# A two-layer recurrent network with routed experts on one core: a new way to pick two experts, one table for exp and log, and the first steps reordered

## The reference, cut to what matters

```python
x = L0_attn_hidden_states                     # 8 x 512 tokens x 128
xn = layernorm(x)
s = L0_attn(xn)      # q, k, v: projection + short conv + silu; then a scan over 32 chunks of 16 tokens
g = silu(L0_moe(xn)) # softmax over 8 logits, top 2 experts, weights p1/(p1+p2), p2/(p1+p2)
x = x + s * g
xn = layernorm(x)
s = L1_ssm(xn)       # state-space scan, 16 states x 256 channels, softplus(delta), exp(delta * A)
g = silu(L1_moe(xn)) # the same routing, but each expert keeps only its first 1.25 * S / 8 tokens
x = x + s * g

# one chunk of the layer-0 scan ("step"); W_in and W_out are 4 x 8 per head, carried on
k_h = softmax(k_t . W_in) * lr;  q_h = softmax(q_t . W_in)
qk = (q_h . k_h) * causal_mask
o_t = q_h . W_out + qk . v_t
W_out = W_out + k_h^T v_t
for _ in range(2):
    g_out = -attn(W_in, k_t, v_t);  g_in = -attn(W_out, v_t, k_t)
    W_in = W_in - lr_in * g_in;     W_out = W_out - lr_out * g_out
```

## Time and profile before

| | us |
|---|---|
| median of 3 runs | 1341.43 |
| lowest, highest | 1332.81, 1348.08 |
| the profiled execution, its own time | 1332.28 |
| span in the profile | 1330.5 |
| DVE busy in the span | 1225.3 (92%) |
| PE, ACT, POOL busy | 1007.2, 720.2, 700.2 |

### The profile page before, as it was taken

How to read it: one execution, slowest core, us unless ns; L and a number is a source line. 1 busy time by engine, 2 the same in 40 slices (tenths; PEclk the granted TensorE clock), 3 DMA queues, 4 the chain that set the end, 5 groups by cost and what they waited for, 6 DMA issues and landing times. The chain is left out here.

```text
span 1330.5 us, 15939 instructions
## 1 busy us (share of the span) xinstructions
PE 1007.2 (76%) x3654; PEld 583.8 (44%) x3655; DVE 1225.3 (92%) x2277; ACT 720.2 (54%) x1364; POOL 700.2 (53%) x637
## 2 busy tenths in 40 slices
PE   4865347887778878887677587569899889898874
PEld 2512334555555555555545542233444444444431
DVE  7997899999999999999997779999989899989999
ACT  5654015555565455654434556446667666766741
POOL 5038732333333333333210027789879778878885
PEclk9687558898999899998877588889999899999988
DMA  9749141000000000000162124464445444443346
GB/s 305 216 119 307 57 134 43 20 24 18 21 24 18 23 18 21 24 18 18 53 203 64 32 107 126 144 177 154 149 146 187 159 136 175 161 155 141 137 150 191
DMA packets 106771, 145.49 MB, mean 109 GB/s; under 512 B 26347, under 2 KB 82424, under 8 KB 101856
## 3 DMA queue, kind: packets, MB, share of 16 engines
q1 hardware_dynamic: 90816, 114.51, 27.2%
q0 software_dynamic: 10240, 25.32, 5.9%
q10 hardware_dynamic: 5664, 5.11, 1.3%
HBM read 112.26 MB, written 39.04 MB: 114 GB/s over the span
## 5 line engine op out<-in xcount | busy, mean ns | idle before, releaser
L2123 DVE TENSOR_TENSOR ps<-ps,cv 128x512 f32<-128x512 f32 x256 | 162.8, 681 | 2.4 <-DMA cv<-bc_scr 2.4
L1161 PE MATMUL ps<-Q,ident 128*128 128x512 f32 x206 | 115.4, 652 | 25.9 <-DVE Q L2141 15.1
L985 PE MATMUL ps<-wd_a,xn 128*128 x576 | 93.8, 312 | 42.7 <-ACT xn L1372 42.7
L1390 ACT ACTIVATE x<-x 128x128 f32<-128x128 f32 (+1 forms) x127 | 32.2, 278 | 140.7 <-DVE x L1981 69.1
L965 PE MATMUL ps<-wg_a,xnT 128*128 x144 | 92.6, 729 | 17.2 <-issue 10.8
L782 POOL DMA_INDIRECT y_tok<-xnT,meta x72 | 72.5, 1006 | 60.6 <-ACT xnT L1378 47.9
L985 PEld LDWEIGHTS ps<-wd_a,xn 128*128 128x128 f32 x576 | 78.9, 212 | 56.3 <-issue 54.8
L995 PE MATMUL ps<-x,ident 128*128 128x64 f32 x512 | 73.6, 296 | 28.8 <-DMA wu_a<-in_wu_a 11.9
L760 POOL DMA_INDIRECT slots_x<-xn,sl_put x64 | 74.9, 1170 | 37.7 <-issue 18.9
L791 POOL TENSOR_TENSOR xn<-xn 128x512 f32<-128x512 f32 x24 | 30.3, 1262 | 122.0 <-DVE x L1944 96.9
L995 PEld LDWEIGHTS ps<-x,ident 128*128 128x128 f32 x512 | 72.9, 217 | 43.2 <-issue 33.1
(11 more groups left out here) (383 smaller groups left out, 3049.1 us busy)
## 6 DMA issues: line engine op xcount, KB each, us to landing
cv<-bc_scr SPq DMA_DIRECT2D x64, 512.0 KB, 3.9
xn<-bc_scr SPq DMA_DIRECT2D x24, 1024.0 KB, 4.7
O<-bc_scr SPq DMA_DIRECT2D x8, 1024.0 KB, 4.9
slots_x<-O POOLq DMA_DIRECT2D x28, 260.0 KB, 5.6
qkv_scr<-wg_a SPq DMA_DIRECT2D x24, 256.0 KB, 3.6
xnT<-slots_x SPq DMA_DIRECT2D x72, 64.0 KB
x<-in_x SPq DMA_DIRECT2D x8, 512.0 KB, 6.5
y_tok<-slots_x SPq DMA_DIRECT2D x2, 2048.0 KB, 13.5
```

The costliest lines, as they stand in the source:

```text
L985: m = pe.matmul(ps[:, 0, 0:D], hidT[:, k, f * P:(f + 1) * P], wd_a[:, bass.ds(off + f * D, D)], start=(f == 0), stop=(f == FC - 1))
L1161: pe.matmul(ps[:, 4, :], ident[:], yc_of(c, n), start=(n == 0), stop=(n == NS - 1)).then_inc(y0_used, 1)
L2123: tt(dBu(g), ps[:, 2 + g, :], b_rows[:, n % 4, :], ALU.mult).then_inc((inject0, b_used)[g], 1)
```

## The change

- **Dispatch.** The two experts are picked from the logits: the row maximum, a one-hot of the first place that has it (`down_e` holds 8 to 1, so that the maximum of mask times `down_e` marks the first), the same again with the first expert pushed down by -3e38. Only the gap between the two maxima is exponentiated (128x32 in place of 128x256), and the weights are 1/(1+e) and e/(1+e). Layer 1 adds a large number to dropped slots instead of multiplying with a kept mask. The expert indices (`texp_i`) are computed behind the slots.
- **One table.** `natural_log_exp_and_others` is loaded where the exp table was, so a log between two exps needs no switch.
- **Projection stage.** `norms` runs in pairs as the squares come; the masks' `ranks(0)` stands between the two halves of the K norms; PE multiplies the units 20 to 23 one by one between the pairs of the Q norms; `unit_length_root(0)` moves behind the convolutions; the gate matmuls have seven banks; V is loaded in three parts.
- **Leading steps.** PE waits for the expert weights only before step 3; POOL makes `op_of` of steps 0 to 3 and `pq_of` of steps 1 to 3, between its scatters, before numbers 5, 16 and 27 of the second 32 (`LEADING`). In step 3 `o_sums` goes ahead of the first expert tiles.
- **Every step.** WO is gone. W_out stays where the running sum leaves it: PP is made from `ends`, the last column of the rows of CS and SC (a stride of 17 numbers, 68 bytes), and one copy (L1940) is left out.
- **Layer 1.** `ranks(1)` goes ahead of the third inner projection.

```diff
+        CS_SC = r.take(2 * DI * HD, CH + 1)
+        CS, SC = CS_SC[:, 0:DI * HD], CS_SC[:, DI * HD:]
+        ends = CS_SC[:, :, CH].rearrange("p (D e) -> p D e", e=HD)
...
-                o.mark(dve.tensor_copy(WO[:, 0, :], CS[:, :, CH]))
-                w_o = o.mark(dve.scalar_tensor_tensor(WO[:, 1, :], GR[:, 3], lr_of(1, c), CS[:, :, CH], ALU.mult, ALU.add))
+                w_o = o.mark(dve.scalar_tensor_tensor(SC[:, :, CH], GR[:, 3], lr_of(1, c), CS[:, :, CH], ALU.mult, ALU.add))
                 dve.wait_ge(v_packed, c + 1)
                 o.wait(w_o)
-                tt(PP, bc(VC, 1, 2 * DI), bc(both(WO[:]), 2, CH), ALU.mult).then_inc(p2_ready, 1)
+                tt(PP, bc(VC, 1, 2 * DI), bc(ends, 2, CH), ALU.mult).then_inc(p2_ready, 1)
...
+                def one_hot(j, src, top):
+                    o.link(tt(eq, src, bc(top, 2, E), ALU.is_equal))
+                    o.link(tt(eq, eq, bc(down_e[:], 1, NT), ALU.mult))
+                    o.link(dve.tensor_reduce(pick, eq, AX_X, ALU.max))
+                    o.link(tt(oh[:, j], bc(down_e[:], 1, NT), bc(pick, 2, E), ALU.is_equal))
+                o.link(dve.tensor_reduce(first, lg, AX_X, ALU.max))
+                one_hot(0, lg, first)
+                o.link(dve.scalar_tensor_tensor(others, oh[:, 0], LOWEST, lg, ALU.mult, ALU.add))
+                o.link(dve.tensor_reduce(second, others, AX_X, ALU.max))
+                tt(gap, second, first, ALU.subtract).then_inc(logits_ready, 1)
+                one_hot(1, others, second)
+                tt(mask, oh[:, 0], oh[:, 1], ALU.add).then_inc(mask_ready, 1)
...
-            for b in range(4, B):
-                project(2 * B + b)
             pe.wait_ge(lr_copied, B)
-            norms(1, sq_q, 7)
+            for k in range(4):
+                project(2 * B + 4 + k)
+                norms(1, sq_q, 7, (k,))
...
-            for b in range(B):
-                silu(2 * B + b)
-                if b < 4:
-                    tap(2 * B + b + 4)
-                k = b - 2
-                if 0 <= k < 4:
-                    if k == 0:
-                        act.wait_ge(q_in, 32)
-                    square(Q, sq_q, 2 * k)
+            act.wait_ge(q_in, 32)
+            for k in range(4):
+                silu(2 * B + k)
+                tap(2 * B + 4 + k)
+                square(Q, sq_q, 2 * k)
+            for b in range(4, B):
+                silu(2 * B + b)
...
                 for i in range(NT):
+                    if j and i in LEADING:
+                        o_product(LEADING.index(i))
+                        q_product(LEADING.index(i) + 1)
...
-            pe.wait_ge(slots_ready, 1)
-            pe.wait_ge(we_loaded, 16 * 3)
...
                 q_sums(c, 4, HD)
+                if after and not here:
+                    o_sums(c)
...
-                    if k == 0:
+                    if k == 0 and (here or not after):
                         o_sums(c)
             with pe.Fori(0, FIRST - 1) as c:
                 step(c, False)
+            pe.wait_ge(slots_ready, 2)
+            pe.wait_ge(we_loaded, 16 * 3)
```

More of the change, by code:

```diff
@@ L548, in op_of, with heads_load @@
             return eng.tensor_tensor(OP, bc(EQ, 2, HD), CS.rearrange("p (D e) l -> p D e l", D=DI)[:, :, :, 1:CH + 1], ALU.mult)
[L550 to L556, removed]
+        def heads_load(eng, lo, hi, w, dst, done):
+            for b in range(lo, hi):
+                eng.wait_ge(stored[b], 16 * ((1, 0, 2).index(w) + 1))
+            eng.dma_start(dst[lo * H:hi * H, :, :],
+                          qkv_scr[w, lo:hi].rearrange("b (h e) t -> (b h) e t", h=H)).then_inc(done, 16)
         block = ctx.enter_context(nc.Block())
@@ L910, in project, with norms @@
                 pe.matmul(ps[:, 2 + cu % 4, :], wproj[:, w * P:(w + 1) * P], xnT[:, b * L:(b + 1) * L], start=True, stop=True).then_inc(proj_ps, 1)
[L912 to L917, removed]
+            def norms(n, sq, bank, pairs):
+                for k in pairs:
+                    pe.wait_ge(squared, 4 * n + k + 1)
+                    for e in (2 * k, 2 * k + 1):
+                        m = pe.matmul(ps[:, bank, :], ident[:], sq[:, e, :], start=(e == 0), stop=(e == HD - 1))
+                if k == 3:
+                    m.then_inc(norm2, 1)
             turn0(0)
@@ L1235, in _ @@
             inner(0, 1)
+            ranks(1)
             pe.wait_ge(conv1_done, 2)
@@ L1316, in _ @@
             silu(2 * B - 1)
-            act.preload_act_table(ACT.Exp)
+            act.wait_ge(k_in, 32)
+            for k in range(2):
+                square(K, sq_k, 2 * k)
+            act.preload_act_table_set(EXP_AND_LOG)
             act.wait_ge(logits_ready, 1)
-            act.activation(route[0].lg, route[0].lg, ACT.Exp).then_inc(probs_ready, 1)
-            act.wait_ge(k_in, 32)
-            for k in range(4):
+            act.activation(best[:, 2, :], best[:, 2, :], ACT.Exp).then_inc(probs_ready, 1)
+            for k in range(2, 4):
                 square(K, sq_k, 2 * k)
@@ L1347, in _ @@
             act.activation(LR[:], LR[:], ACT.Ln, bias=1.0).then_inc(lr_log, 1)
-            act.wait_ge(lr_stored, 16)
-            for b in range(B):
-                act.wait_ge(gate_ps, b + 1)
-                act.activation(gateT[:, b * L:(b + 1) * L], ps[:, 2 + b % 4, :], ACT.Copy).then_inc(gate_copied, 1)
-            act.preload_act_table(ACT.Exp)
-            act.wait_ge(v_in, 32)
+            for b in range(3, B - 1):
+                gate(b)
+            act.preload_act_table_set(EXP_AND_LOG)
+            gate(B - 1)
             temper = HD ** -0.5
@@ L1420, in step @@
                     exp(E2, rec_2, exp_2, temper)
-                if after:
+                if after and here:
                     xT(c + 1, 0)
@@ L1431, in step @@
                     y(c, 0)
+                if after and not here:
+                    xT(c + 1, 0)
                 if after:
@@ L1747, in dispatch @@
-                o.wait()
-                tt(mask, oh[:, 0], oh[:, 1], ALU.add).then_inc(mask_ready, 1)
+                eq, others = prod[:, 0], prod[:, 1]
+                first, second, gap, pick = (best[:, n, :] for n in range(4))
+                def one_hot(j, src, top):
[3 more added lines that the diff above has]
+                    o.link(tt(oh[:, j], bc(down_e[:], 1, NT), bc(pick, 2, E), ALU.is_equal))
@@ L1858, in _, with step @@
             tt(E3[:, DI:2 * DI, :], SK, bc(M3[:, DI:2 * DI], 2, CH), ALU.subtract).then_inc(rec_3, 1)
-            def step(c, routed, first=False, last=False, alone=False, early=None, late=None):
+            def step(c, routed, first=False, last=False, early=None, late=None):
                 ts = bass.ds(c * CH, CH)
@@ L1874, in step @@
                 o.wait(o.n)
-                if alone:
+                if first:
                     pq_of(dve, c).then_inc(pq_ready, 1)
@@ L1982, in step @@
                 gated(2)
-            dve.wait_ge(v_in, 32)
-            PER_R = PER_P = 27
-            step(0, False, first=True, alone=True)
+            dve.wait_ge(v_in, 48)
+            PER_R = PER_P = 26
+            step(0, False, first=True)
             for lo, hi, routed in ((1, FIRST, False), (FIRST, AFTER, True)):
@@ L1991, in _ @@
                     o.loop(c, first - lo * per, per)
-                    step(c, routed, alone=not routed)
+                    step(c, routed)
                 o.end(first, per, hi - lo)
```

146 lines of the change are left out of this document (70 added, 76 removed).

## The result

The changed kernel takes 1349.05 us (median of 20 runs, 1344.09 to 1354.28) against 1338.29 for the kernel before (20 runs, 1329.66 to 1348.08): ratio 1.0082, 95% interval 1.0065 to 1.0099, 11 us slower. The forecast was 1337 us. The time lies in its range and within 1%, but the sum said 4.5 us less and the runs say 11 us more; that difference of some 15 us is what the rest explains.

What follows compares the result with a forecast made beforehand. DVE was taken to bound the steps, so edits count on its chain. Terms +21 - 3 + 1 - 12.5 - 3 + 3.5 - 3 - 8.5 = -4.5 us, put on the median 1341.4: 1337 us, range 1317 to 1350.

Steps and rivals of the forecast that it cites:

- PP read in place: In each step PP reads W_out at a 68-byte stride: +21 us, the copy left out -3, strided updates +1.
- The order of w_c and h_k: In every step w_c now stands ahead of h_k; the prediction had no term for this.
- First stage: Before step 0, convolutions and gate copies end earlier and step 0's wait for expert weights goes: -12.5 us.
- the closed circle of the units 20 to 23: Before step 0, tap, square, norms and next projection form rounds of 4.6 us; convolutions end at 98.3: -4.3 us.
- Rival 2: Circle of units 21 to 23 with PE at its lower level, rounds of 7.2 us: +3.5, 1345 us; chance 0.17.
- Leading steps: Before step 4, four `op_of` and three `pq_of` leave DVE, which then waits for ACT's exp: -3 us.
- Step 3 to 4: In step 3 ACT's copies for the first tiles stand ahead of step 4's exp: +3.5 us.
- -3 for dispatch: In layer 1 mask, ranks and slots get shorter, the softplus chain loses two loads and the ranks: -3 us.
- -8.5 for the rows: In layer 1's rows, four of six DVE stalls for exp lose at most 2.56 us each: -8.5 us (3 to 10).
- Rival 3: Table switches are worth 2.66 us each, with a drain of 1.38: -10, 1331 us; chance 0.07.

Runs made afterwards that it cites:

- e3: The changed kernel with the strided operand kept and h_k ahead of w_c again: 1342.29 us, ratio 1.0057 to the kernel before.
- e5: On the changed kernel with packed WO and old order (ratio 0.9876), POOL's products of the first four steps moved among the scatters: 1321.18 us, ratio 0.9894.
- e8: On the changed kernel with packed WO and old order (ratio 0.9876), step 3's old order of exp, first tiles and o sums: 1317.24 us, ratio 0.9856.
- e10: The changed kernel without the table set in the rows of the second layer: 1353.96 us, ratio 1.0139 to the kernel before.
- e4: The changed kernel with the products of the first four steps on DVE again, POOL making none between its scatters: 1345.57 us, ratio 1.0070.

## Why the prediction was wrong

By its own steps, the forecast in us, then what was measured:

- **PP read in place, +21 - 3 + 1 = +19**: right. PP at 1903 ns for 1.90; all three together 17 us by the ratios, 19 by the step.
- **The order of w_c and h_k, nothing**: this is the step that failed. The full diff has it, the swapped lines and a new `o.wait(w_c)` (the cut diff above leaves them out), and the prediction gives it no term. It costs 0.32 us in a step, 10 us: some 6 are the wait that reading in place forces on x_k, and so part of the price of the term above, and 4 are a swap that nothing forced (e3). By the sequencer's records both are dear because a register instruction for the address stands behind the wait. Together with the term above a routed step was forecast at 19.0 us and is 19.37.
- **First stage, -12.5**: right, mechanism and size. Step 0 starts 6.4 to 7.8 us earlier and the 5.4 us wait is gone; the closed circle of the units 20 to 23 has its forecast round. Rival 2 (a circle at PE's low clock) did not come: the granted clock from 85 to 120 us was 0.86, not 0.70. Its price was read wrong, too: at the low level the row it names has 2.06 us for two records, 1.03 and not 0.85 each, so that a round would have taken 8.1 us and not 7.2 (6 x 1.03 + 1.9).
- **Leading steps, -3**: wrong in sign. Three instructions stretched by 2.76, 1.72 and 1.21 us eat the 4.8 us of the seven products, and DVE waits 0.38 us for exp in three steps. Taking it back gave 1.6 and 2.4 us by the ratios, 3 us by the profiles. I had asked only whether POOL would be late. The Trainium skill (SBUF — State Buffer, "Who interferes with whom") says that a VectorE instruction with two SBUF inputs contends with a GpSimd one that reads SBUF, and that `tensor_reduce` does not; the rows of the changed kernel and of e5 agree, and with that rule the sign of the term would have been open.
- **Step 3 to 4, +3.5**: right in kind and near in size: the wait is 2.9 us. Taking it back (e8) gave 2.7 us by the ratios and 2.6 by the profile up to step 4, but only 0.4 up to step 31, so the net size is between 0.4 and 3 us.
- **Layer 1, -3 for dispatch and -8.5 for the rows**: the two together are 5 to 7 us, and nearly all of it is the table set. The -3 came, but from the set: without it (e10) the way from logits to scan is 27.1 us, as before. The shorter dispatch gave 0.4 us there, and DVE waits 8.3 us for the softplus instead of 2.7 in e10:

```profile
DVE K L2120 <- ACT V L1632: 8.3, 1, 8.3
```

  The rows gave some 2 to 4 us of the forecast 8.5. It counted each load as if the exp behind it were released by nothing else; the exps are released by PE's low-rank product too. The forecast took the 15.0 us of one row of waits down to 6; that row is 10.4, and all four rows together stayed at 21.

Sum with the measured sizes: +17 + 10 - 12 + 2 + 3 - 6 = +14 (with the step 3 term at its most), against 11 and 13.5 measured (1.0082 and 1.0101). Of the 18 us between this sum and the forecast's, 10 are the order, 5 the leading steps and 5 the loads, less 2 for PP. That the time still lies in the range is luck: its slow end was there for rival 2 (1345 to 1350 us), which did not come, and nothing in it stood for the order.

Rival 3 falls by its price. In both kernels every load in the rows starts 17 to 19 ns behind the ACTIVATE ahead of it and takes 1.28 us, and the next ACTIVATE, where it has nothing else to wait for, starts 11 to 12 ns behind it. So a switch is 1.31 us here, and the drain of 1.38 us that the Trainium skill adds (ScalarE: Activation LUTs, "What ACT_TABLE_LOAD costs") does not show.

## What to carry to other kernels

On an engine that is busy 96% of a stage, an edit of the order of small dependent instructions is an edit of the time: look, for each instruction, whether the one directly ahead of it makes its input, and whether its own address is computed behind that wait. Saving a copy by reading and writing in place can cost twice, in the strided operand and in the new write-after-read wait (x_k must not overwrite what w_c still reads); this change paid a third time for a swap that it didn't need. And before work is moved from DVE to POOL, look at what DVE does at that moment: beside reductions the products here were free for DVE, beside products of two SBUF tiles each cost DVE 1.1 to 1.7 us for a length of 1.1 to 1.2.

## What the hardware showed

- A DVE TENSOR_TENSOR beside a POOL TENSOR_TENSOR lasts until 0.10 us (64 elements) or 1.1 us (1024 elements) behind its end: 1.37 us for 0.22, 2.94 and 3.98 for 1.22. It stands as one long busy row, and no wait names it. By the starts of the records DVE's instruction began first each time (137.00 against 137.64), and it was still the one that was held.
- POOL's scatters beside the same DVE instructions don't stretch them (e4: longest 1218 ns of 31).
- An operand read at every 17th element costs 0.66 ns an element more in a 1024-element TENSOR_TENSOR (1903 for 1225 ns), close to the 0.68 at 128 bytes (L1756) and at 2 KB (L1851).
- In these steps a DVE instruction that waits for the one directly ahead of it starts 0.03 us behind its end, or 0.13 to 0.17 us where a register instruction for its address (0.04 to 0.08 us) stands behind the wait. One that waits for nothing new starts 0.08 us ahead of the end of the one before it (L1897: 409.89 against 409.97).
- A table load of ACT takes 1.28 us and leaves 0.03 us idle around it; 16 loads fewer lowered ACT's busy time by 22.5 us and the time of the kernel by 5 to 6.
